# A four-layer cross-attention decoder on one core: the third layer's heads of 96 rows packed into tiles of 128

## The reference

```python
B, Q, D = (8, 64, 512); CTX = 512
H, KV, HD = (16, 4, 96)
hidden = jnp.concatenate([context, latents], axis=1)
q = (latents @ Wq.T).reshape(b, q_len, H, HD)
k = (hidden @ Wk.T).reshape(b, s_len, KV, HD)
v = (hidden @ Wv.T).reshape(b, s_len, KV, HD)
scores = jnp.einsum('bkgqd,bksd->bkgqs', q, k) * scale
attn = jax.nn.softmax(scores, axis=-1)
out = jnp.einsum('bkgqs,bksd->bkgqd', attn, v)
return out.reshape(b, q_len, H * HD) @ Wo.T
```

## Time and profile before

| | |
|---|---|
| median of 3 runs | 2134.17 us (2130.99 to 2135.35) |
| the profiled execution | 2134.03 us, its span 2132.1 us |
| TensorE busy | 1966.9 us (92%), 10874 matmuls |
| VectorE busy | 1428.9 us (67%) |
| ScalarE busy | 1035.1 us (49%) |
| GpSimd busy | 951.7 us (45%) |
| mean granted TensorE clock | 0.966 |
| chain that ended last | PE 70%; DVE 15%; issue 7%; ACT 6%; POOL 2% |

### The profile page before, as it was taken

One profiled execution on the slowest core, in us unless ns is written; L12 is line 12 of the kernel. 1 busy time (PEld: TensorE's weight loads), 2 busy tenths in 40 slices (PEclk: granted clock), 3 DMA queues, 4 the chain that ended last, 5 costly groups with the idle time before them and its releaser, 6 DMA issues.

```text
span 2132.1 us, 33124 instructions
## 1 busy us (share of the span) xinstructions
PE 1966.9 (92%) x10874; PEld 1653.4 (78%) x10874; DVE 1428.9 (67%) x2532; ACT 1035.1 (49%) x2268; POOL 951.7 (45%) x975
## 2 busy tenths in 40 slices
PE   5999999999748999998988999998799999999997
PEld 4788888888537888886766888887588888888886
DVE  5777777777768878887234555556466776677676
ACT  3766676666315545543123544542255555455442
POOL 2655555554536656663322332323154444344532
PEclk9999999999869999999988999999899999999999
DMA  3212222221301111111210101001110110111001
GB/s 141 75 46 81 84 74 78 57 74 55 99 35 54 56 54 52 61 48 51 73 48 4 34 15 28 23 1 56 55 32 30 45 46 22 40 45 45 16 20 46
DMA packets 47068, 106.76 MB, mean 50 GB/s; under 512 B 6064, under 2 KB 21936, under 8 KB 43104
## 3 DMA queue, kind: packets, MB, share of 16 engines
q1 hardware_dynamic: 46944, 105.14, 15.7%
HBM read 98.37 MB, written 6.75 MB: 49 GB/s over the span
## 4 chain that ended last, share of the span: by engine, by line
PE 70%; DVE 15%; issue 7%; ACT 6%; POOL 2%; DVEq 0%; ACTq 0%; POOLq 0%
PE psX L370 24%; PE psQ L370 12%; PE psS L370 12%; PE psO L370 11%; PE psT L755 6%; PE psT L370 1%; DVE pT_lo L913 1%; DVE p_sb L897 1%; DVE nbias L901 1%; ACT pT_hi L1099 1%; ACT dq_space L449 1%; ACT p_sb L1088 1%; DVE nbias L891 1%; PE psX L825 1%; ACT p_sb L1092 1%
## 5 line engine op out<-in xcount | busy, mean ns | idle before, releaser
L1213 POOL TENSOR_SCALAR p_sb<-p_sb,rrec 128x512 f32<-128x512 f32 (+1 forms) x320 | 267.0, 834 | 690.2 <-DVE rrec L909 690.2
L1099 ACT ACTIVATE pT_hi<-psT 128x512 fp32r<-128x512 f32 (+2 forms) x384 | 234.9, 612 | 349.6 <-PE psT L755 348.0
L913 DVE TENSOR_TENSOR pT_lo<-psT,pT_hi 128x512 fp32r<-128x512 f32 (+2 forms) x384 | 270.9, 705 | 107.0 <-ACT pT_hi L1099 106.4
L370 PE MATMUL psO<-pT_hi,v_hi 128*128 128x256 f32 (+1 forms) x832 | 254.6, 306 | 24.1 <-DVE pT_lo L913 18.1
L755 PE MATMUL psT<-ident,p_sb 128*128 128x128 f32 x1600 | 244.9, 278 | 14.2 <-POOL p_sb L1213 10.7
L755 PEld LDWEIGHTS psT<-ident,p_sb 128*128 128x128 f32 x1600 | 197.4, 143 | 52.8 <-POOL p_sb L1213 15.8
L370 PE MATMUL psO<-pT_lo,v_hi 128*128 128x256 f32 (+1 forms) x832 | 237.3, 285 | 0.0
L370 PE MATMUL psO<-pT_hi,v_lo 128*128 128x256 f32 (+1 forms) x832 | 237.1, 285 | 0.0
L370 PE MATMUL psQ<-xnT_hi,wq_hi 128*128 128x512 f32 (+1 forms) x448 | 189.3, 422 | 14.8 <-DVE qscr L875 9.2
L370 PE MATMUL psS<-kT_hi,q_hi 128*128 128x512 f32 (+2 forms) x448 | 177.1, 395 | 18.0 <-ACT p_sb L1092 16.1
L1092 ACT ACTIVATE p_sb<-psS,nbias 128x512 f32<-128x512 f32 (+1 forms) x192 | 145.3, 757 | 81.0 <-DVE nbias L903 81.0
(11 more groups left out here) (337 smaller groups left out, 4750.7 us busy)
## 6 DMA issues: line engine op xcount, KB each, us to landing
wq_f<-in_a_wq SPq DMA_DIRECT2D x96, 256.0 KB, 2.7
wo_f<-in_a_wo SPq DMA_DIRECT2D x24, 1024.0 KB, 5.7
wkv_f<-in_a_wkv SPq DMA_DIRECT2D x24, 512.0 KB, 3.8
mask_sb<-in_codes SPq DMA_DIRECT2D x32, 174.0 KB, 2.4
qscr<-in_amax SPq DMA_DIRECT2D x32, 174.0 KB, 2.3
w<-qscr SPq DMA_DIRECT2D x32, 174.0 KB, 1.8
wo_f<-in_f_wT SPq DMA_DIRECT2D x3, 1024.0 KB, 5.2
wq_f<-in_a_wq SPq DMA_DIRECT2D x16, 192.0 KB, 2.4
```

The costliest lines, as they stand in the source:

```text
L370: mm = pe.matmul(dst, w, m, start=(first and k == 0), stop=(last and k == n - 1))
L913: L.t_lo.inc(dve.tensor_tensor(pT_view(L, pT_lo, j), t_view(L, j), pT_view(L, pT_hi, j).bitcast(F32), ALU.subtract))
L1099: L.t_hi.inc(act.activation(pT_view(L, pT_hi, j), t_view(L, j), ACT.Copy))
L1213: L.s_norm.inc(pool.tensor_scalar(p_view(L, j), p_view(L, j), rrec[:, j:j + 1], 1.0, ALU.mult, ALU.mult))
```

## The change

For heads of fewer than 128 rows (`packed`: the third layer alone) the four heads of a group make three tiles of 128 rows. Tile t holds head t in rows 0 to 95 and rows 32t to 32t+31 of head 3 in rows 96 to 127. The host orders the columns of Wq and the rows of Wo that way, so the weights come as three blocks of 128 in place of four of 96.

- `q_proj` makes three query tiles a group, in slots (2,3), (3,3) and (0,3); slot (1,3) has none. `q_high` and `q_low` each get a second instruction, ahead of the one for 96 rows, that moves psQ's rows 96 to 127 into head 3's query (`q_last`): for even groups in `q_even`, which shares its place with mask_sb, for odd ones in place 3 of oT_hi/oT_lo.
- `scores` of head 3 wait for the third query tile.
- `o_high` and `o_low` of head 3 are three instructions each (`o_parts`), one for each 32 rows of psO; the semaphore goes up after the last.
- The output product of a tile of 128 rows is 9 matmuls over three tiles of 128 rows. Every tile of it, the first `end` tile too, waits for o_lo of all four heads.
- The plan: output tiles in (0,2), (0,3) twice, and (1,0); k1 from (1,2) to (1,3), k2 from (2,0) to (2,1), v0 to (2,2), t0 to (2,3).
- The weight splits follow: three for wq and three for wo. `f2_sync` also waits for the first transposes of the last group, before its loads into mask_sb, vecs and wo_f.

```diff
+OUT_PACKED = {(0, 2): [0], (0, 3): [1, 2], (1, 0): [3]}
+SPLIT_PACKED = dict(wq=[(h, 2) for h in range(4)], wkv=[(0, 1), (0, 3)], wo=[(1, 1), (1, 3), (2, 3)])
...
     dict(kind="plain", hd=96, groups=4, keys=768, slots=4, nbuf=1, ahead=1, settle=1, q_slot=(3, 3, 3, 3),
-         outs=OUT_EARLY, splits=SPLIT_TILES,
-         prep={(1, 1): ["k0"], (1, 2): ["k1"], (2, 0): ["k2"], (2, 1): ["v0"], (2, 2): ["t0"],
+         outs=OUT_PACKED, splits=SPLIT_PACKED,
+         prep={(1, 1): ["k0"], (1, 3): ["k1"], (2, 1): ["k2"], (2, 2): ["v0"], (2, 3): ["t0"],
                (3, 0): ["v1"], (3, 1): ["t1", "v2"], (3, 2): ["t2"]}),
...
+        self.packed = self.hd < P
+        self.tiles = 3 if self.packed else G4
+        self.wide = P if self.packed else self.hd
...
+    def query(self, g, h, d):
+        to = self.head(g, h, d)
+        return to if to and to[1] < self.tiles else None
+
+    def buffer(self, g, t):
+        return (self.tiles * g.par + t) % 2
...
+        with nc.sbuf_tensor("q_even", [P, 2, TOK], F32R) as q_even:
+            pass
...
+        q_last = [[q_even[:, z, :] for z in (0, 1)], [z[:, G4 - 1, :] for z in (oT_hi, oT_lo)]]
...
+        def o_parts(L, g, h):
+            if h == L.tiles:
+                return [(psO[32 * t:32 * t + 32, :], *(z[L.hd:P, t, :] for z in (oT_hi, oT_lo))) for t in range(L.tiles)]
+            return [(psO[0:L.hd, :], *(oT_view(L, z, g, h)[0:L.hd] for z in (0, 1)))]
+
+        def q_view(L, g, h):
+            if h < L.tiles:
+                return [z[0:L.hd, L.buffer(g, h), :] for z in (q_hi, q_lo)]
+            return [z[0:L.hd] for z in q_last[g.par]]
...
             def scores(g, h, j):
                 if j == 0:
-                    L.q_lo.wait(pe, g.at(4, h + 1))
+                    L.q_lo.wait(pe, g.at(L.tiles, min(h + 1, L.tiles)))
...
                 if kind in ("out", "end"):
-                    L.wo_lo.wait(pe, gp.at(4, 4))
-                    for h in range(G4):
+                    L.wo_lo.wait(pe, gp.at(L.tiles, L.tiles))
+                    for h in range(L.tiles):
                         if h == 0 or what == ("end", 0):
-                            L.o_lo.wait(pe, gp.at(4, h + 1 if kind == "end" else 4))
+                            L.o_lo.wait(pe, gp.at(4, h + 1 if kind == "end" and not L.packed else 4))
...
             def q_low(g, h):
+                if L.packed:
+                    at = slice(32 * h, 32 * h + 32)
+                    last_hi, last_lo = (z[at] for z in q_last[g.par])
+                    dve.scalar_tensor_tensor(last_lo, psQ[hd:P, :], L.scale, last_hi.bitcast(F32), ALU.mult, ALU.subtract)
...
             def o_low(g, h):
                 L.o_hi.wait(dve, g.at(4, h + 1))
-                L.o_lo.inc(dve.tensor_tensor(oT_view(L, 1, g, h), psO[0:hd, :], oT_view(L, 0, g, h).bitcast(F32),
-                                             ALU.subtract))
+                for src, hi, lo in o_parts(L, g, h):
+                    ins = dve.tensor_tensor(lo, src, hi.bitcast(F32), ALU.subtract)
+                L.o_lo.inc(ins)
...
             def q_high(g, h):
+                        act.activation(q_last[g.par][0][32 * h:32 * h + 32], psQ[hd:P, :], ACT.Copy, scale=L.scale)
                         ins = act.activation(dst, psQ[0:hd, :], ACT.Copy, scale=L.scale)
...
             def o_high(g, h):
-                L.o_hi.inc(act.activation(oT_view(L, 0, g, h), psO[0:hd, :], ACT.Copy))
+                for src, hi, _ in o_parts(L, g, h):
+                    ins = act.activation(hi, src, ACT.Copy)
+                L.o_hi.inc(ins)
...
         def f2_sync(sp, L):
-            L.wo_lo.wait(sp, 4 * L.n)
+            L.wo_lo.wait(sp, L.tiles * L.n)
+            L.t_mm.wait(sp, L.group_slots * (L.n - 1) + 1)
```

More of the change, by code:

```diff
@@ L240, in place @@
     def place(self, g, h):
-        return G4 if h == 0 and g.par and self.outs is not OUT_EARLY else h
+        return G4 if h == 0 and g.par and self.outs is OUT_PAIRS else h
 def walk(eng, L, prologue, head, tail):
@@ L631, in w_low @@
             else:
-                L.wo_hi.wait(pool, g.at(4, piece + 1))
+                L.wo_hi.wait(pool, g.at(L.tiles, piece + 1))
                 L.wo_lo.inc(pool.tensor_tensor(lo, f, hi.bitcast(F32), ALU.subtract))
@@ L652, in load_wq @@
             def load_wq(g, h):
[L653 to L657, removed]
+                k = g.at(L.tiles, h)
+                L.wq_lo.wait(sp, g.at(L.tiles, h - 1))
+                b = L.buffer(g, h)
+                L.wq_dma[b].inc(sp.dma_start(wq_f[:, b, 0:DC * L.wide], names["wq"][k, :, :]), 16)
             def load_wkv(g):
@@ L719, in q_proj @@
             def q_proj(g, h):
-                L.wq_lo.wait(pe, g.at(4, h + 1))
-                (L.q_f if L.rope else L.q_lo).wait(pe, g.at(4, h) if g.off or g.loop is not None or h else 0)
-                L.q_mm.inc(three(pe, psQ[0:hd, :], [
-                    ([z[:, h % 2, c * hd:(c + 1) * hd] for z in (wq_hi, wq_lo)],
+                L.wq_lo.wait(pe, g.at(L.tiles, h + 1))
+                (L.q_f if L.rope else L.q_lo).wait(pe, g.at(L.tiles, h) if g.off or g.loop is not None or h else 0)
+                n, b = L.wide, L.buffer(g, h)
+                L.q_mm.inc(three(pe, psQ[0:n, :], [
+                    ([z[:, b, c * n:(c + 1) * n] for z in (wq_hi, wq_lo)],
                      (xnT_hi[:, c, :], xnT_lo[:, c, :])) for c in range(DC)]))
@@ L1045, in head @@
                         dq_vector(dve, g, h, "low" if j == 1 else "high")
-                    if j == L.q_slot[h] and L.head(g, h, L.q_lead):
-                        (q_front if L.rope else q_low)(*L.head(g, h, L.q_lead))
+                    if j == L.q_slot[h] and L.query(g, h, L.q_lead):
+                        (q_front if L.rope else q_low)(*L.query(g, h, L.q_lead))
                     for u in L.slot_uses(g, h, j):
@@ L1176, in head @@
                         row_exp(*nxt)
-                    if j == L.q_slot[h] and L.head(g, h, L.q_lead) and not L.rope:
-                        q_high(*L.head(g, h, L.q_lead))
+                    if j == L.q_slot[h] and L.query(g, h, L.q_lead) and not L.rope:
+                        q_high(*L.query(g, h, L.q_lead))
                     if j == 0 and L.rope and L.head(g, h, 2):
```

70 lines of the change are left out of this document (40 added, 30 removed).

## The result

The changed kernel takes 2143.37 us (median of 5, 2141.73 to 2145.75) against 2134.17 (a median of 5 as well, not of 3 as the table before has it): ratio 1.0046, 95% interval 1.0033 to 1.0058. That is 9.2 us slower; +11 was forecast. The profiled execution of the changed kernel took 2141.73 (span 2139.7, clock 0.962), the quickest of its five, 7.6 us of span above the profile before.

What follows compares the result with a forecast made beforehand. TensorE bounds the kernel (busy 100 of 100 us); packing exposes VectorE's queue at boundaries. Sum: -8.2 - 8.2 + 0.6 + 1.0 + 20.1 + 1.3 + 1.2 + 3.3 = +11.1 us, so 2145.1; range 2129 to 2152.

Steps and rivals of the forecast that it cites:

- The boundary: Between groups, from T (scores of (0,0) start): row max (0,2) behind o_low; stall 5.0 plus clock 1.7, three times: +20.1 us.
- The rival with short pieces: VectorE's queue at the boundary: 32-row instructions take a third, stall 2.9 us, too short for the clock; 2129.6; chance 0.08.
- The full gain: Whole layer: all 96 saved matmuls are gained, 21.9 us, giving 2112.2; chance 0.05.
- The case with no fall: At the boundaries: the stall comes but the clock doesn't fall; +3.0 us, 2137.0; chance 0.17.
- Group 0 and the prologue: q_low delay of 1.3 us: +1.3 in the prologue, +1.2 in group 0, where nothing follows slot (0,3)'s query product.
- The last group: Group 3, where nothing is prepared: (1,3) without its query product becomes a bare slot; +5.0 us in the stretch table.
- The bare pair (1,3)+(2,0): Last group: 8.31 us now, priced at the 9.31 of the already bare pair (2,1)+(2,2): +1.0, not -2.74.
- The end of the layer: First tile's matmuls no longer run while head 3 is taken out, nine begin at half clock; last add later: +3.3 us.
- the clock stays down: After each boundary the clock stays at half, up to 8.4 us lost instead of 1.7: +20, 2165; chance 0.08.

Runs made afterwards that it cites:

- fill_more: Changed kernel with fifteen matmuls of 512 columns without use added in slot (0,1) of groups 1 to 3: 2142.51 us, ratio 1.0042.
- moved_only: Kernel before with its 12-matmul output tiles moved to (0,2), (0,3) twice and (1,0), heads not packed: 2141.36 us, ratio 1.0036.
- fill: Changed kernel with nine matmuls of 512 columns without use added in slot (0,1) of groups 1 to 3: 2142.22 us, ratio 1.0042.
- max_first: Changed kernel with head 3's o_low behind the row max, pT_low and reciprocal of slot (0,1) on VectorE: 2137.96 us, ratio 1.0017.
- one_piece: Changed kernel with head 3's result taken out by one 32-row instruction each on ScalarE and VectorE, not three; output not the reference's: 2135.31 us, ratio 1.001.
- outs_back: Changed kernel with its 9-matmul output tiles begun in slot (0,1) again, as (0,1), (0,2), (0,3), (1,0): 2132.88 us, ratio 1.0001.
- query_in_gap: Changed kernel with TensorE's query product of tile 2 in slot (0,1) instead of (0,3): 2135.11 us, ratio 1.0007.
- both edits: Changed kernel with the query product of tile 2 in slot (0,1) and head 3's o_low behind the row max: 2127.9 us, ratio 0.9971.
- the end filled: Changed kernel with query product and o_low both moved, plus matmuls without use at the third layer's end (8, then 3, 6, 2 before transposes): 2120.77 us, ratio 0.9937.

## Why the prediction was right, and where it was not

**The boundary: right, step by step.** Pieces of 32 rows cost what 96 rows cost: 0.69 and 0.59. Row maximum (0,1) at T+2.75 (forecast 2.74), scores (0,2) at 4.77 (4.77), row maximum (0,2) at 8.68 (8.35), scores (0,3) at 10.72 (10.4), rest 3.77 (3.7). The 0.3 too little lie on ScalarE: o_high starts at T+4.74 (4.61), and its pieces start 0.60 apart, not 0.49. The 0.49 of the earlier trace rows was one pair of instructions; other copies of 512 columns with no idle time between them mostly start 0.48 to 0.59 apart, so one row was too few to take a spacing from. The clock fell at all three boundaries, in both profiles of the change. Its price is 1.3 to 1.6 us (fill_more, moved_only), not 1.7. The forecast made +1.4 of a group; +1.6 and +1.5 came.

The rival with short pieces fell with the first row of 0.69. The full gain fell with the 3.77 of rest. The case with no fall was half alive. Counted over the three boundaries of each profile: behind rests of 3.8 us the clock fell at 6 of 6 (the change, twice), behind rests of 1.7 to 1.8 us at 6 of 15 (fill, moved_only, max_first, one_piece, outs_back), and where no rest was above 1.0 us at 0 of 12 (query_in_gap, fill_more, both edits, the end filled). (TensorE: Matmul & The Clock Gate, section Part 1: The HAM clock gate, of the Trainium skill has the gate follow how busy TensorE has been recently. The counts fit that as far as they go; max_first and one_piece, alike on TensorE for 9 us and unlike in the clock, show that it is not enough to say at which boundary the clock falls.)

**Group 0 and the prologue: each right in sign, the sum not.** -1.7 together against a forecast of 0.0. The layer's first row maximum lies anywhere from 1130.4 to 1136.4 among the kernels, so +0.6 against +1.3 says nothing; that group 0 got 1.0 more than forecast does. 0.3 of it are the wait behind its query product, taken at +1.2 (slot (1,0) takes 4.77 us instead of 3.82, the next slots 0.1 less). 0.6 are the slot (0,2), 6.05 us instead of 6.68: the half clock of the layer's start ends in it, at 1149.7 after and at 1150.4 before.

**The last group: the term that was mis-sized.** +5.0 forecast, +2.1 measured. The bare pair (1,3)+(2,0) was priced at the 9.31 of its neighbour; it took 7.79 (scores at 1427.11 and 1434.90), less than the 8.31 before. That is 1.5 us of the 2.9 missed. The rest are a later slot, 5.68 us before (scores at 1442.71 and 1448.38) and 4.15 after (1447.97 and 1452.12): one fall fewer among the bare slots. The neighbour's 9.31 held a fall of the clock too. Falls come here behind 1416, 1433, 1444 and 1461 before, and behind 1422, 1439, 1456 and 1470 after, and nothing in the rests says where. A price of a bare slot has to be read without the fall in it.

**The end of the layer: right.** +2.9 against +3.3. TensorE rests 4.09 us ahead of the nine matmuls, which begin at half clock (0.43 apart) and end at full.

**Behind the layer: missed.** The sum ended at the last add, as if what follows were the same work shifted. It isn't: the clock falls at 1484.2, between the transposes of the normalised tiles, and stays at 0.50 until 1497.8 although TensorE hardly rests. Busy time by stretch in the changed kernel:

```profile
1484.20:1497.80 13.60, 13.33 (x60) 12.59 (x58) 11.76 (x21) 3.50 (x7) 6.07 (x4) 0.50 0.00 1
```

13.6 us at half clock can lose half of that, 6.8; +6.3 came. The same place in the kernel before, the transposes and the first and last of the 48 matmuls:

```profile
1477.36 0.66 PE L537 MATMUL psS<-ident,xn_f 128*128 128x128 f32 x4 [1.58 <-DVE xn_f L496]
1478.41 0.66 PE L537 MATMUL psS<-ident,xn_f 128*128 128x128 f32 x4 [0.40 <-DVE xn_f L496]
...
1478.82 0.31 PE L370 MATMUL psT<-kx_hi,xnT_hi 128*128 128x136 f32 x1
...
1484.10 0.28 PE L370 MATMUL psS<-kx_lo,xnT_hi 128*128 128x136 f32 x1
```

The 48 take 5.28 us there and 10.07 after. That the clock is the cause, the filled end shows: 67.54 with nothing changed against both edits but matmuls in the rests. Why the clock falls is not shown. The rests between the transposes are nearly the same, 1.58 and 0.40 before, 0.19, 1.61 and 0.27 after; yet all nine profiles of packed kernels with these rests unfilled have the 13.6 us at half clock, and none of the four profiles of unpacked kernels. Nine matmuls a tile change what lies between and ahead of the rests; which part of that counts stays open. It is the cost of the rival "the clock stays down", at a place that none of the steps looked at, and with TensorE busy where the rival had it resting.

**The fourth layer: missed, and it hid the other.** -5.1: of these -3.6 are VectorE's two waits at the loop's jumps. The last 1.6 are a fall of the clock near the end of the program that this execution lacks: the other profile of the changed kernel has 42.92 us behind its last row maximum, the kernel before 42.89, this one 41.27. So against the median of 2143.37 it is execution scatter.

So 2143.4 against 2145.1 is closer than the reasons deserve. To its last add the layer made +6.4 where +11.1 was forecast; +6.3 and -3.6 behind it were in no term of the sum. Without the chance that 16 more VectorE instructions take the waits away the change would be some 3.6 us slower still (an estimate from the two groups). The nearness of the total is luck: what was missed in group 3 and in group 0, and the fourth layer, make up for what was missed behind the layer.

**What the change lacked.** The packing saves 1.8 us a group if the output tiles stay where they were; their move takes 3.4 away (82.1 to 85.5, the fall of the clock included). To gain from packing, what is bare must be covered with useful work (query_in_gap, 4.1 a group), and the three pieces must stand behind the row maximum (both edits, 1.4 more): 80.0 a group against 84.0 before. (Trainium Kernel Development and Optimization, section Best Practices, of the Trainium skill asks for tiles of 128 partitions. The traces bear out that full tiles save matmuls, 96 of them; what the fuller tiles cost to take out of PSUM, where one extraction of 0.59 + 0.69 became three, the gain doesn't cover at the place where it stood.)

## What to carry to other kernels

Before filling TensorE's tiles, count what takes them out of PSUM: the cost of a ScalarE or VectorE instruction that moves 512 columns doesn't depend on its rows here (0.59 and 0.69 us with 32 as with 96), and its place ahead of a row maximum decides what it costs. Where one matmul tile covers a round of softmax, moving it away cost more here (3.4 us a group) than the packing gave (1.8); put other useful work there first. And a sum over the changed stretch isn't enough: look at the rests of TensorE behind it as well, and at how far a half clock reaches from there.

## What was not expected of the hardware

- The half clock lasted 13.6 us (1484.2 to 1497.8) with TensorE busy 13.33 us of it, most of it in matmuls of 136 columns 0.21 apart; it came back while matmuls of 512 columns followed. At the boundaries it lasted 3.4 us, once 6.8 (max_first).
- Equal rests (0.78 and 1.78 us) and equal matmuls for 9 us, unequal clocks: fallen in max_first, not in one_piece. Open.
- 16 small VectorE instructions more took waits of 2.83 and 2.71 us (for issue) out of a later loop whose code is unchanged, with 10 packets fewer on an instruction queue; the median fell by 3.4 us.
- On ScalarE, the three pieces of 32 rows start 0.60 apart, two instructions of 0.59 in the earlier trace rows 0.49: back to back doesn't mean one spacing. What sets it was not tried.
